# Half of the clipped products of a dense attention made on GpSimd, with a third buffer of exponentials

## The chip, the cores and the metric

One core of one Trainium2 chip. The metric is the device time of the kernel in microseconds (us). The core has five engines with queues of their own: TensorE (PE in the profile, PEld for its weight loads), VectorE (DVE), ScalarE (ACT), GpSimd (POOL) and SyncE (SP). They are ordered among each other by semaphores alone.

## The reference

Four graph networks in a row on 3125 nodes with 64 features and 100000 edges. Only the last one matters here, an attention over the edges:

```python
h = _leaky_relu(feats)
z = h @ W
el, er = z @ attn_l, z @ attn_r
e = _leaky_relu(el[src] + er[dst])                      # leaky with slope 0.2
emax = jax.ops.segment_max(e, dst, num_segments=n)
ex = jnp.exp(e - emax[dst])
denom = jax.ops.segment_sum(ex, dst, num_segments=n)
alpha = ex / jnp.where(denom == 0, 1.0, denom)[dst]
rst = jax.ops.segment_sum(alpha[:, None] * z[src], dst, num_segments=n)
return rst + bias
```

## The kernel before

Earlier phases compute the first three networks and leave in SBUF `adj3`, a dense table of edge counts: for each block of 128 source nodes (25 blocks, index `sx`), how many edges lead from each of the 128 sources (partitions) to each of the 3200 padded destination nodes (columns), in bf16. The last phase, the one that is changed, makes the attention dense: it goes through all pairs of source and destination, and the count of a pair is its weight, zero where there is no edge.

The destinations are cut into 5 chunks of 640 columns (`NCH`, `CW`), index `i`. Each chunk has 25 steps, one for each source block, so a step has the number t = 25 i + sx, from 0 to 124. A step runs over four engines:

- ScalarE (L1499, L1502) makes two exponentials of 128 x 640: `E1[t % 2]` in PSUM, of el + er minus the maximum, and `E2[t % 2]` in SBUF, of the same with the slope of 0.2. The first waits until the larger of step t - 2 is made (`mx`), the second until the product of step t - 2 is made (`mu`).
- VectorE, `larger(t)` (L1601): `E2 = max(E1, E2)`, which is the exponential of the leaky sum. One input is in PSUM, the other in SBUF.
- VectorE, `counted(t)` (L1609): `XB[t % 2] = min(E2, 2) * adj3`, both inputs in SBUF, f32 and bf16, the result f32. It waits until TensorE is done with step t - 2 (`mm`), since XB has two buffers.
- TensorE (L1539): five products of a 128 x 128 piece of XB with the 65 columns of `Z[:, sx]` (64 features and a one), added up in PSUM over the 25 steps of the chunk. In the profile each is two records, 10 a step.

Beside the steps VectorE prepares the next chunk's maxima, spread over the first 22 steps (`TURN`): `maximum(i + 1, v)` (L1574) is a running maximum MN of min(counts, a scaled el), both inputs in SBUF, 25 of them on 22 steps, so that three steps have two. In step 22 `reduce_maxima` (L1580 to L1583) reduces what TensorE has transposed (L1517, `turn_maxima`), TensorE spreads the result again (L1523, L1524, `spread_maxima`), and in step 23 `shifts` (L1592 to L1595) makes the next chunk's inputs to the exponentials. TensorE has these in a fixed order between its steps: transposes before step 21, spread before step 22. `divide` (L1616 to L1621) finishes the previous chunk in step 2.

VectorE's order in a step is written out by hand: product of step t - 1, then the maxima, then the larger of step t. GpSimd has one instruction in the whole phase, the addition of the bias (L1488).

The lines about the changed part:

Of the kernel before, what the change touches and what calls it, by code (L numbers as in the profile page):

```python
# [5 lines left out]
P = 128  # L6
NB = (N + P - 1) // P
# [39 lines left out]
f32, i32, u16, bf16 = mybir.dt.float32, mybir.dt.int32, mybir.dt.uint16, mybir.dt.bfloat16  # L47
ALU = mybir.AluOpType
ACT = mybir.ActivationFunctionType
# [27 lines left out]
@contextmanager  # L77
def phase(nc, names):

    with ExitStack() as c:  # L80
        sems = {n: c.enter_context(nc.semaphore(n)) for n in names.split()}
        with nc.Block() as block:
            yield block, sems
        nums = sorted(s.num for s in sems.values())
        at = [k for k in range(len(nums)) if not k or nums[k] != nums[k - 1] + 1] + [len(nums)]
        for k in range(len(at) - 1):
            nc.gpsimd.sem_clear(range(nums[at[k]], nums[at[k + 1] - 1] + 1))
        nc.all_engine_barrier()
# [9 lines left out]
def share(n, k, of):  # L98

    return range(n * k // of, n * (k + 1) // of)  # L100
# [27 lines left out]
def build(nc, a, out):  # L128
# [9 lines left out]
    with ctx:  # L138
        sb = lambda n, s, d: ctx.enter_context(nc.sbuf_tensor(n, s, d))
        LOW, HIGH = NB * NP // 2, 8400  # L140
        arena = sb("arena", [P, LOW + HIGH], f32)
        adj3 = arena[:, 0:LOW].bitcast(bf16).rearrange("p (s n) -> p s n", n=NP)
        al = sb("al", [P, 784], f32)
        e32 = sb("e32", [P, NB, D32], f32)
# [2 lines left out]
        identz = sb("identz", [P, 2 * P], bf16)  # L147
        identb = identz[:, 0:P]
        stage = sb("stage", [P, 2000], f32)
        adj_t = nc.dram_tensor("edge_counts", (P, NB * NP), bf16).ap()  # L150
        ps = ctx.enter_context(nc.psum_tensor("ps", [P, 8 * 512], f32))
        got = [ctx.enter_context(nc.semaphore(f"gathered{k}")) for k in range(LEAD)]
# [3 lines left out]
        def V(off, *shape, dt=f32, parts=P):  # L156

            n = 1
            for s in shape:
                n *= s  # L160
            words = n if dt in (f32, i32) else (n + 1) // 2
            v = arena[0:parts, off:off + words]
            if dt != f32:
                v = v.bitcast(dt)
            if n % 2 and dt not in (f32, i32):
                v = v[:, 0:n]
            if len(shape) == 2:
                v = v.rearrange("p (a b) -> p a b", b=shape[1])
            if len(shape) == 3:
                v = v.rearrange("p (a b c) -> p a b c", b=shape[1], c=shape[2])  # L170
            return v

        def A(off, *shape, dt=f32, parts=P):

            return V(LOW + off, *shape, dt=dt, parts=parts)
# [1283 lines left out]
        CW = 5 * P  # L1459
        NCH, TURN = 5, 22  # L1460
        E1 = [ps[:, 1024 * k:1024 * k + CW] for k in range(2)]
        MEL = ps[:, 2048:2048 + CW]
        EOS = [ps[:, 3072 + 512 * k:3072 + 512 * k + 5 * (D + 1)] for k in range(2)]
        E2 = [e32[:, :, :].rearrange("p a b -> p (a b)")[:, 0:CW], A(6450, CW)]
        X1 = [ERT[:, CW * k:CW * (k + 1)] for k in range(NCH)]
        X2 = [A(6450 + CW * (1 + k), CW) for k in range(2)]
        XB = [A(CW * k, CW) for k in range(2)]
# [3 lines left out]
        MC, OC, LIM, SPAN = [al[:, o:o + n] for o, n in ((770, 5), (776, 5), (781, 2), (783, 1))]  # L1471
        EL2, SEL = A(1600, NB), e32[:, :, :].rearrange("p a b -> p (a b)")[:, CW:CW + NB]
        LIMS = e32[:, :, :].rearrange("p a b -> p (a b)")[0:1, 700:702]
        with phase(nc, "lim lims limb sel mn1 st mn t1 dg t2 xr ex mx mu mm oc bl b3 wr") as (block, s):
            @block.sync
            def _(sp):
                sp.dma_start(B3, a["L3_gnn_bias"].rearrange("(o n) -> o n", o=1).to_broadcast([P, D])).then_inc(s["bl"], 16)
# [7 lines left out]
            @block.gpsimd  # L1485
            def _(pool):
                pool.wait_ge(s["bl"], 16)
                pool.tensor_tensor(XS, XS, B3.unsqueeze(1).to_broadcast([P, NB, D]), ALU.add).then_inc(s["b3"], 1)  # L1488

            @block.scalar  # L1490
            def _(act):
                act.wait_ge(s["sel"], 1)
                for i in range(NCH):
                    act.wait_ge(s["xr"], i + 1)
                    for sx in range(NB):
                        t = i * NB + sx
                        if t >= 2:
                            act.wait_ge(s["mx"], t - 1)
                        act.activation(E1[t % 2], X1[i], ACT.Exp, bias=EL[:, sx:sx + 1])  # L1499
                        if t >= 2:  # L1500
                            act.wait_ge(s["mu"], t - 1)
                        act.activation(E2[t % 2], X2[i % 2], ACT.Exp, bias=EL2[:, sx:sx + 1]).then_inc(s["ex"], 1)  # L1502

            @block.tensor
            def _(pe):
                pe.wait_ge(s["lim"], 1)
                for q in range(2):
                    ins = pe.transpose(ps[0:1, 3072 + q * P:3072 + (q + 1) * P], LIM[:, q:q + 1], identf[:, :])
                ins.then_inc(s["lims"], 1)
                pe.wait_ge(s["limb"], 1)  # L1510
                pe.matmul(ps[:, 3584:3586], ONE[0:1, :], LIMS, start=True, stop=True).then_inc(s["lims"], 1)

                def turn_maxima(i):

                    pe.wait_ge(s["mn"], NB * (i + 1))
                    for c in range(5):
                        ins = pe.transpose(MEL[:, c * P:(c + 1) * P], MN[:, c * P:(c + 1) * P], identf[:, :])  # L1517
                    ins.then_inc(s["t1"], 1)

                def spread_maxima(i):  # L1520

                    pe.wait_ge(s["dg"], i + 1)
                    pe.matmul(MEL[:, 0:512], ONE, DGN[:, 0:512], start=True, stop=True)  # L1523
                    pe.matmul(MEL[:, 512:CW], ONE, DGN[:, 512:CW], start=True, stop=True).then_inc(s["t2"], 1)  # L1524

                turn_maxima(0)
                spread_maxima(0)
                for i in range(NCH):
                    for sx in range(NB):
                        t = i * NB + sx  # L1530
                        if i + 1 < NCH and sx == TURN - 1:
                            turn_maxima(i + 1)
                        if i + 1 < NCH and sx == TURN:
                            spread_maxima(i + 1)
                        if sx == 0 and i >= 2:
                            pe.wait_ge(s["oc"], i - 1)
                        pe.wait_ge(s["mu"], t + 1)
                        for c in range(5):
                            ins = pe.matmul(EOS[i % 2][:, c * (D + 1):(c + 1) * (D + 1)], XB[t % 2][:, c * P:(c + 1) * P], Z[:, sx],  # L1539
                                            start=sx == 0 and c == 0, stop=sx == NB - 1, skip_group_check=True)  # L1540
                        ins.then_inc(s["mm"], 1)

            @block.vector
            def _(dve):
                st = Steps(dve, s["st"])
# [17 lines left out]
                def clear(i):  # L1563

                    if i:
                        dve.wait_ge(s["t2"], i)
                    dve.memset(MN, 0.0).then_inc(s["mn1"], 1)  # L1567
# [30 lines left out]
                def larger(t):  # L1598

                    dve.wait_ge(s["ex"], t + 1)  # L1600
                    dve.tensor_tensor(E2[t % 2], E1[t % 2], E2[t % 2], ALU.max).then_inc(s["mx"], 1)  # L1601

                def counted(t):

                    i, sx = t // NB, t % NB
                    dve.wait_ge(s["mx"], t + 1)
                    if t >= 2:
                        dve.wait_ge(s["mm"], t - 1)
                    dve.scalar_tensor_tensor(XB[t % 2], E2[t % 2], 2.0, adj3[:, sx, i * CW:(i + 1) * CW], ALU.min, ALU.mult)\  # L1609
                        .then_inc(s["mu"], 1)  # L1610

                def divide(i):
# [15 lines left out]
                for i in range(NCH):  # L1628
                    nxt = i + 1 < NCH
                    if nxt:  # L1630
                        clear(i + 1)
                    for sx in range(NB):
                        t = i * NB + sx
                        if t:
                            counted(t - 1)
                        if i and sx == 2:
                            divide(i - 1)
                        if nxt and sx < TURN:
                            for v in share(NB, sx, TURN):
                                maximum(i + 1, v)  # L1640
                        if nxt and sx == TURN:
                            reduce_maxima(i + 1)
                        if nxt and sx == TURN + 1:
                            shifts(i + 1)
                        larger(t)
                counted(NCH * NB - 1)
                divide(NCH - 1)

# [35 lines left out]
```

## Time and profile before

| | |
|---|---|
| Median of 3 runs | 4718.8 us (4710.01 to 4724.73) |
| Profiled execution: span from the first to the last instruction | 4719.8 us |
| Last phase, in the span | from about 4340 us to the end |
| First step (first L1601) | 4384.8 us |
| Last chunk's first step | 4655 us |
| Mean granted TensorE clock from 4384 to 4720 us | 0.51 |

The profile gives no time of the profiled execution apart from its span; the span is 1.0 us above the median of the runs. It is read here by its groups of instructions (duration and idle time of each line) and, for the order within a step, by its timeline. A share of busy time over the whole span says nothing on this phase, which is 8% of it.

### The profile page before, as it was taken

The numbers are of one execution on the slowest core, as the hardware profiler recorded it, in microseconds if no ns is written. First come the engines' busy times: TensorE is split into PE (matmuls) and PEld (weight loads), VectorE is DVE, ScalarE is ACT, GpSimd is POOL, SyncE is SP. The second block draws the span as 40 slices with busy tenths as digits, with TensorE's granted clock in tenths as the row PEclk, the third lists the DMA queues.
The fourth block names the chain that finished last, engine by engine and source line by source line (L and its number), as shares of the span: only waits on it lengthen the run. The fifth ranks groups of instructions, "written<-read, shape, count | busy, mean of one in ns | idle before, by whom it ended". The sixth has DMA issues, their size and how long they took to land. (4 is left out here: it accounts for less than half of the span.)

```text
span 4719.8 us, 91070 instructions
## 1 busy us (share of the span) xinstructions
PE 3468.1 (73%) x24128; PEld 3020.2 (64%) x24128; DVE 3236.7 (69%) x10293; ACT 2427.2 (51%) x8514; POOL 2503.7 (53%) x2592
## 2 busy tenths in 40 slices
PE   3767666666667776666656777777775799996789
PEld 2556555555555555555555766767675799996788
DVE  7677767677657777677764777778785433354998
ACT  0766666666275766666627666656542100000555
POOL 5777777676277777777617777777752100000000
PEclk9687888888667878888866888888875899997555
DMA  3344444444143444444414444444423200000000
GB/s 78 100 101 104 106 113 122 113 121 110 51 99 96 109 103 115 114 120 121 111 49 98 103 105 104 104 99 108 101 63 105 94 2 2 2 1 1 2 3 3
DMA packets 576845, 384.28 MB, mean 81 GB/s; under 512 B 421913, under 2 KB 498833, under 8 KB 576343
## 3 DMA queue, kind: packets, MB, share of 16 engines
q1 hardware_dynamic: 373463, 151.17, 12.5%
q0 software_dynamic: 81344, 84.68, 9.8%
q10 hardware_dynamic: 121536, 142.57, 9.8%
q8 instruction: 213, 3.49, 0.3%
q14 instruction: 289, 2.37, 0.2%
HBM read 312.87 MB, written 65.24 MB: 80 GB/s over the span
## 5 line engine op out<-in xcount | busy, mean ns | idle before, releaser
L617 POOL DMA_INDIRECT arena<-node_table,arena x1660 | 1601.7, 965 | 604.4 <-issue 474.0
L772 PE MATMUL ps<-arena 128*128 128x129 f32 x4980 | 943.9, 320 | 187.1 <-DVE arena L922 103.0
L681 ACT ACTIVATE arena<-arena 128x129 f32<-128x129 f32 x2490 | 742.7, 300 | 451.2 <-DVE arena L890 443.9
L772 PEld LDWEIGHTS ps<-arena 128*128 128x128 f32 x4980 | 788.0, 225 | 274.0 <-DVE arena L922 138.0
L919 DVE TENSOR_SCALAR arena<-arena 128x128 f32<-128x128 uint16 x2490 | 883.3, 361 | 88.7 <-PE ps L772 37.8
L617 POOL DMA_INDIRECT arena<-last_node_table,arena x830 | 793.2, 956 | 281.6 <-issue 235.3
L890 DVE TENSOR_TENSOR arena<-ps,arena 128x258 f32<-128x258 f32 x1245 | 524.7, 421 | 591.2 <-PE ps L761 244.8
L1208 PE MATMUL ps<-arena 128*128 128x192 bf16 x6875 | 587.0, 247 | 12.7 <-DVEq L1368 4.9
L1208 PEld LDWEIGHTS ps<-arena 128*128 128x128 bf16 x6875 | 584.7, 98 | 14.6 <-issue 7.4
L761 PE MATMUL ps<-arena 128*128 x2496 | 503.4, 335 | 106.1 <-ACT e L671 37.6
L761 PE MATMUL ps<-arena,e 128*128 x2484 | 494.6, 331 | 110.5 <-DVE arena L890 52.2
L798 PE MATMUL ps<-stage,al 128*128 128x400 bf16 x1190 | 357.0, 387 | 259.2 <-ACT al L689 111.6
L761 PEld LDWEIGHTS ps<-arena 128*128 128x128 f32 x2496 | 423.4, 233 | 173.1 <-issue 156.4
L761 PEld LDWEIGHTS ps<-arena,e 128*128 128x128 f32 x2484 | 410.5, 228 | 179.6 <-issue 162.7
L681 ACT ACTIVATION_READ_ACCUMULATOR arena<-arena 128x1 f32 x2490 | 468.2, 188 | 0.0
L932 DVE TENSOR_TENSOR arena<-arena,ps 128x129 f32 (+1 forms) x1245 | 363.6, 292 | 119.4 <-issue 50.5
L668 ACT ACTIVATE arena<-arena 128x256 f32<-128x256 bf16 x624 | 313.1, 502 | 138.0 <-PE ps L761 40.2
L668 ACT ACTIVATE e<-arena 128x256 f32<-128x256 bf16 x621 | 310.4, 500 | 112.3 <-PE ps L761 38.6
L1488 POOL TENSOR_TENSOR stage<-stage 128x1600 f32<-128x1600 f32 x1 | 3.6, 3552 | 656.3 <-DMA stage<-in_L_gnn_bias 656.3
L908 DVE TENSOR_SCALAR stage<-arena 128x400 bf16<-128x400 uint16 x1190 | 343.2, 329 | 0.0
L1539 PE MATMUL ps<-arena 128*128 128x65 f32 x1250 | 289.5, 420 | 33.8 <-DVE arena L1609 33.8
L1539 PEld LDWEIGHTS ps<-arena 128*128 128x128 f32 x1250 | 273.0, 329 | 51.0 <-DVE arena L1609 50.3
(338 smaller groups left out, 4625.5 us busy)
## 6 DMA issues: line engine op xcount, KB each, us to landing
arena<-in_attr SPq DMA_DIRECT2D x1245, 96.0 KB, 2.2
arena<-slot_rows ACTq DMA_DIRECT2D x249, 320.0 KB
edge_counts<-al ACTq DMA_DIRECT2D x397, 100.0 KB
arena<-node_table,arena POOLq DMA_INDIRECT x1660
edge_counts<-stage ACTq DMA_DIRECT2D x198, 100.0 KB
arena<-last_node_table,arena POOLq DMA_INDIRECT x830
arena<-edge_counts SPq DMA_DIRECT2D x24, 500.0 KB
stage<-edge_counts SPq DMA_DIRECT2D x16, 500.0 KB
```

Of the source, the lines that this page charges most:

```text
L617: pool.indirect_dma_start(out=RING[:, t % R_SLOTS, XO:XO + XG], out_offset=None, in_=table[:, :], in_offset=bass.IndirectOffsetOnAxis(ap=I ...
L668: act.activation(o, ROWB[r % 2][:, (j % 5) * BT * P:(j % 5 + 1) * BT * P], ACT.Square, bias=pid1, scale=-1.0)\
L681: ins = act.activation(PR[j % 3][:, q], PR[j % 3][:, q], ACT.Copy, accum_out=AL[w % 2][:, c:c + 1])
L761: ins = pe.matmul(UPS[j % 2][:, q * AB:(q + 1) * AB], OHT[j % 6][:, q * P:(q + 1) * P], U[:, bass.ds(b, 1), :].rearrange("p a b -> p (a b) ...
L772: ins = pe.matmul(BPS[j % 2][:, 0:AB], WOH[j % 2][:, q], RING[:, r + q, D32:D32 + AB], start=q == 0, stop=q == BT - 1)
L798: ins = pe.matmul(WPS, LOH[k % 3][:, q], KOH[k % 3][q], start=q == 0, stop=t == 0 and q == G4 - 1)
L890: dve.tensor_tensor(PR[j % 3], UPS[j % 2].rearrange("p (a b) -> p a b", b=AB), RING[:, r:r + BT, D32:D32 + AB], ALU.mult).then_inc(s["pr"], 1)
L908: ins = dve.tensor_scalar(KOH[k % 3][q], iota1[:, 0:NB * WIN], KEY4[:, adj0 + k, q:q + 1], None, ALU.is_equal)
L919: ins = dve.tensor_scalar(WOH[j % 2][:, q], iota1[:, 0:P], DZT[:, t:t + 1], PT[w % 2][:, c:c + 1], ALU.is_equal, ALU.mult)
L932: dve.tensor_tensor(to, to, BPS[j % 2], ALU.add).then_inc(s["add"], 1)
L1208: last = pe.matmul(ps[:, o + 256 * c:o + 256 * c + 3 * D], adj3[:, sx, bass.ds((d0 + c) * P, P)], g3[:, sx].rearrange("p a b -> p (a b)"), ...
L1539: ins = pe.matmul(EOS[i % 2][:, c * (D + 1):(c + 1) * (D + 1)], XB[t % 2][:, c * P:(c + 1) * P], Z[:, sx], start=sx == 0 and c == 0, stop= ...
```

## The change

Products of odd steps move from VectorE to GpSimd, where each is two operations: a clip to between 0 and 2 in place in E2 (`tensor_scalar`), a wait for it (`cl`), and the product with the counts (`tensor_tensor`), which writes `XB[1]` and increments `mp`. VectorE keeps the even ones, which all go to `XB[0]` and increment `mu`. E2 gets a third buffer, and ScalarE's second exponential waits for the product of step t - 3, whichever engine makes it. TensorE waits for `mp` or `mu` by the parity of the step.

```diff
+        third = sb("third", [P, 640], f32)
...
-        E2 = [e32[:, :, :].rearrange("p a b -> p (a b)")[:, 0:CW], A(6450, CW)]
+        E2 = [e32[:, :, :].rearrange("p a b -> p (a b)")[:, 0:CW], A(6450, CW), third[:, :]]
...
             def _(pool):
                 pool.wait_ge(s["bl"], 16)
                 pool.tensor_tensor(XS, XS, B3.unsqueeze(1).to_broadcast([P, NB, D]), ALU.add).then_inc(s["b3"], 1)
+                for t in range(1, NCH * NB, 2):
+                    i, sx = t // NB, t % NB
+                    pool.wait_ge(s["mx"], t + 1)
+                    pool.tensor_scalar(E2[t % 3], E2[t % 3], 2.0, 0.0, ALU.min, ALU.max).then_inc(s["cl"], 1)
+                    pool.wait_ge(s["cl"], t // 2 + 1)
+                    if t >= 2:
+                        pool.wait_ge(s["mm"], t - 1)
+                    pool.tensor_tensor(XB[1], E2[t % 3], adj3[:, sx, i * CW:(i + 1) * CW], ALU.mult).then_inc(s["mp"], 1)
...
+                def rows_free(t):
+
+                    if t >= 3:
+                        act.wait_ge(s["mp"] if (t - 3) % 2 else s["mu"], (t - 3) // 2 + 1)
+
...
-                        if t >= 2:
-                            act.wait_ge(s["mu"], t - 1)
-                        act.activation(E2[t % 2], X2[i % 2], ACT.Exp, bias=EL2[:, sx:sx + 1]).then_inc(s["ex"], 1)
+                        rows_free(t)
+                        act.activation(E2[t % 3], X2[i % 2], ACT.Exp, bias=EL2[:, sx:sx + 1]).then_inc(s["ex"], 1)
...
-                        pe.wait_ge(s["mu"], t + 1)
+                        pe.wait_ge(s["mp"] if t % 2 else s["mu"], t // 2 + 1)
...
-                    dve.tensor_tensor(E2[t % 2], E1[t % 2], E2[t % 2], ALU.max).then_inc(s["mx"], 1)
+                    dve.tensor_tensor(E2[t % 3], E1[t % 2], E2[t % 3], ALU.max).then_inc(s["mx"], 1)
...
-                    dve.scalar_tensor_tensor(XB[t % 2], E2[t % 2], 2.0, adj3[:, sx, i * CW:(i + 1) * CW], ALU.min, ALU.mult)\
+                    dve.scalar_tensor_tensor(XB[0], E2[t % 3], 2.0, adj3[:, sx, i * CW:(i + 1) * CW], ALU.min, ALU.mult)\
                         .then_inc(s["mu"], 1)
...
-                        if t:
+                        if t % 2:
                             counted(t - 1)
```

## Rows read from the trace of the kernel before

**Rows 1.** The page: span, and the lines of the chain that ended last.

```profile
span 4719.8 us, 91070 instructions
...
PE ps L1539 3%; DVE al L1574 1%; DVE e L1601 1%; DVE arena L1601 1%; DVE arena L1609 0%; PE ps L1523 0%; PE ps L1517 0%; DVE al L1593 0%; DVE al L1592 0%; DVE arena L1594 0%; DVE arena L1595 0%; DVE e L1560 0%; DVE al L1567 0%; PE ps L1524 0%; DVE arena L1619 0%
```

**Rows 2.** Groups from 4160 us on: busy us, mean ns of one | idle before, releaser.

```profile
L1539 PE MATMUL ps<-arena 128*128 128x65 f32 x1250 | 289.5, 420 | 33.8 <-DVE arena L1609 33.8
...
L1574 DVE SCALAR_TENSOR_TENSOR al<-arena,e,al 128x640 f32<-128x640 bf16 x125 | 110.0, 880 | 3.9
L1499 ACT ACTIVATE ps<-arena,dis 128x640 f32<-128x640 f32 x125 | 99.7, 797 | 105.1 <-DVE arena L1601 52.9 <-DVE e L1601 52.3
L1502 ACT ACTIVATE e<-arena 128x640 f32<-128x640 f32 x63 | 52.1, 828 | 9.9 <-DVE arena L1609 7.1
```

**Rows 3.** Timeline, VectorE in one step with an M: start us, duration us.

```profile
4389.61 0.82 DVE L1601 TENSOR_TENSOR e<-ps,e 128x640 f32<-128x640 f32 x1
4390.46 0.83 DVE L1609 SCALAR_TENSOR_TENSOR arena<-e,arena 128x640 f32<-128x640 f32 x1
...
4391.20 0.88 DVE L1574 SCALAR_TENSOR_TENSOR al<-arena,e,al 128x640 f32<-128x640 bf16 x1
...
4392.00 0.82 DVE L1601 TENSOR_TENSOR arena<-ps,arena 128x640 f32<-128x640 f32 x1
```

**Rows 4.** Timeline and windows of TensorE in the last chunk (busy us, count, clock).

```profile
4657.16 57.86 PE L1539 MATMUL ps<-arena 128*128 128x65 f32 x270 [3.49 <-DVE arena L1609]
...
4655.00:4720.00 65.00, 57.86 (x270) 57.67 (x270) 45.08 (x63) 38.48 (x50) 0.00 (x0) 0.51 0.02 5
```

**Rows 5.** GpSimd by line (ns min/median/max), by timeline (L1488) and by group (L328).

```profile
L624 POOL TENSOR_TENSOR arena<-arena x15: 723/724/949, 1238.0 to 3601.2; 128x320 f32<-128x320 f32 x15
...
L625 POOL TENSOR_TENSOR arena<-arena x15: 747/751/877, 1238.8 to 3602.0; 128x320 f32<-128x320 f32 x15
...
L1119 POOL COPY arena<-arena x8: 1847/1854/3245, 3620.6 to 3680.1; 128x2000 bf16<-128x2000 bf16 x8
...
4343.10 3.55 POOL L1488 TENSOR_TENSOR stage<-stage 128x1600 f32<-128x1600 f32 x1 [656.30 <-DMA stage<-in_L_gnn_bias]
...
L328 POOL TENSOR_SCALAR_AFFINE_SELECT identz<-identz 128x128 bf16<-128x128 bf16 x1 | 0.4, 408 | 0.0
...
L328 POOL TENSOR_SCALAR_AFFINE_SELECT identf<-identf 128x128 f32<-128x128 f32 x1 | 0.3, 292 | 0.2 <-POOL identz L325 0.2
```

**Rows 6.** Timeline at a convolution's end, VectorE and GpSimd at once.

```profile
1242.22 0.75 POOL L625 TENSOR_TENSOR arena<-arena 128x320 f32<-128x320 f32 x1
...
1242.62 0.49 DVE L1021 TENSOR_TENSOR arena<-ps,arena 128x320 f32<-128x320 f32 x1 [4.30 <-PE ps L861]
1243.15 0.72 POOL L624 TENSOR_TENSOR arena<-arena 128x320 f32<-128x320 f32 x1 [0.18 <-POOL arena L625]
...
1243.25 0.97 DVE L1024 TENSOR_TENSOR arena<-arena 128x320 f32<-128x320 f32 x1
...
1243.95 0.88 POOL L625 TENSOR_TENSOR arena<-arena 128x320 f32<-128x320 f32 x1
1244.26 0.76 DVE L1028 TENSOR_SCALAR arena<-arena 128x320 f32<-128x320 f32 x1
...
1248.30 0.49 DVE L1024 TENSOR_TENSOR arena<-arena 128x320 f32<-128x320 f32 x1
```

**Rows 7.** Timeline of TensorE and VectorE in the turn of chunk 3.

```profile
4645.84 1.27 PE L1517 MATMUL ps<-identf,al 128*128 128x128 f32 x5
4646.15 0.82 DVE L1609 SCALAR_TENSOR_TENSOR arena<-e,arena 128x640 f32<-128x640 f32 x1
...
4647.15 0.82 DVE L1580 TENSOR_REDUCE al<-ps 128x5 f32<-128x640 f32 x1 [0.17 <-PE ps L1517]
...
4649.46 2.08 PE L1523 MATMUL ps<-al 128*128 128x512 f32 x2
...
4652.00 0.82 DVE L1592 TENSOR_TENSOR al<-ps,arena 128x640 f32<-128x640 f32 x1 [1.00 <-PE ps L1524]
```

More of the change, by code:

```diff
@@ L1473, in build @@
         LIMS = e32[:, :, :].rearrange("p a b -> p (a b)")[0:1, 700:702]
-        with phase(nc, "lim lims limb sel mn1 st mn t1 dg t2 xr ex mx mu mm oc bl b3 wr") as (block, s):
+        with phase(nc, "lim lims limb sel mn1 st mn t1 dg t2 xr ex mx mu mp cl mm oc bl b3 wr") as (block, s):
             @block.sync
```

## The prediction

> **What bounds the kernel now.** I read the page first: one execution with a span of 4719.8 us, and a chain that ends in the last phase, with the sums of L1539, the maxima of L1574, the larger exponential of L1601 and the clipped product of L1609 [rows 1]. The change lies wholly in that phase, so nothing of the earlier phases can move. I then took the groups of the phase [rows 2] and the timeline. Three engines run in a ring, 125 times. Call the steps t = 0..124. For a step, ScalarE makes two exponentials, L (L1601, VectorE) takes the larger, C (L1609, VectorE) clips and multiplies it, TensorE sums it in 10 recorded matmuls; in the first 22 steps of chunks 0 to 3 VectorE also makes M (L1574), the running maximum of the next chunk.
>
> In such a step with one M, VectorE starts L at 4389.61, C 0.85 us later, M 0.74 after C, and the next L 0.80 after M: 2.39 us a step, no gap [rows 3]. ScalarE needs 0.80 + 0.83 us, TensorE 2.14 (57.86 us for 270 matmuls, 27 steps) at the granted clock of 0.51, which is the 1.2 GHz level [rows 2, 4]. So VectorE bounds the steps with an M, with TensorE only 0.25 us behind it, and TensorE bounds the last chunk, where it has no gap over those 57.86 us [rows 4].
>
> **What the change removes.** 62 of the 125 C go from VectorE. Of these, 44 are in steps with an M (88 such steps in four chunks), 12 in the last chunk, 6 in the turns between chunks. Where VectorE is the bound a pair of steps (o odd, e even) would fall from 2 x 2.39 = 4.78 us to 4.78 - 0.74 = 4.04. TensorE allows no less than 2 x 2.14 = 4.28.
>
> **What it adds on GpSimd.** For each odd step a clip (one input, 640 columns), a wait for its own end, and a product (two inputs, of which one is bf16). The product: 320 columns take 724 and 751 ns (medians), 1600 take 3.55 us, so 2.2 ns a column above 320, and 640 columns come to 0.74 + 320 x 0.0022 = 1.44 us [rows 5]. Its upper bound: the one operation on GpSimd with both a bf16 and a f32 form took 408 against 292 ns for 128 columns, 0.9 ns a column, which on 640 would make 2.0 us [rows 5]. The clip has no row. The nearest single-input row is the copy of 2000 columns in 1.854 us, 0.93 ns a column: 0.59 us, and some 0.1 for its start, 0.70 us; the lower bound is 0.59, the upper that of a product, 1.44. I take 0.70, since a clip reads one tensor as the copy does. Between one GpSimd instruction and the next that waits for it I take 0.08 us (the product that ends at 1243.87 is followed by one at 1243.95) [rows 6].
>
> The Trainium skill, GPSIMD Engine Reference, section 3.1, gives 1.03 cycles per element at 1.2 GHz for bodies of up to two operations. By that the clip is an estimated 0.55 us, and the pair below 0.15 us shorter; no row here shows a clip.
>
> **The port.** The rows that decide are those of the end of a convolution, where GpSimd and VectorE work at once [rows 6]. L1024, a VectorE operation with two SBUF inputs, takes 0.49 us alone (1248.30) and 0.97 when it starts 0.10 after a GpSimd product; it ends at 1244.22, 0.35 us after that product's end at 1243.87. L1028 stretches in the same way to 0.76. L1021, with one input from PSUM, starts inside a GpSimd product (1242.22 to 1242.97) and takes 0.49, what L1024 takes alone for the same size. The GpSimd product that starts at 1243.95, while L1024 is still at work, takes 0.88 instead of 0.75. (L1028 has one SBUF input, and a GpSimd product holds it too.) So a VectorE operation with two SBUF inputs and a GpSimd product don't overlap; 0.14 us of VectorE's start are hidden in the wait (0.49 - 0.35). Here C (E2 and the counts) and M (the counts and MN) have two SBUF inputs, L (PSUM and E2) has not.
>
> The Trainium skill, SBUF — State Buffer, section "SBUF: two separate sides", says that the pair of ports is held exclusively for a whole instruction, and the loser fully blocks. The trace agrees on the blocking but shows 0.14 us of the start hidden; with nothing hidden the pair below would be 5.42 and not 5.28 us.
>
> **The pair afterwards.** Put time 0 at the end of a product on GpSimd for which C waits. C is done at 0.69 (0.83 - 0.14), M starts at 0.60, L(o) at 1.40, M at 2.25, L(e) at 3.05, and VectorE comes to the next C at 3.90. GpSimd: the clip of o is issued at about 2.3, when L(o) is done, but M, which stands directly behind L on VectorE, has the port till 3.13. Clip to 3.83 or, with some of its start hidden, 3.76; product from 3.84. Who is first at 3.9? C(e) also waits for TensorE to be done with the only even XB: the odd step's matmuls can start at 0.05, take 2.14, the even one's another 2.14, so C is not free before 4.37. The product wins by half a microsecond, holds the port to 5.28, and C waits for it. The pair is thus 5.28 us: VectorE's 4.04, and 1.44 for the product, less the 0.14 hidden and some overlap. In words: a C of 0.74 us is taken off VectorE and a blockade of 1.44 us, during C, is put on it. ScalarE has slack (3.26 us in the pair; the third E2 lets it run ahead, and the odd product is done before its buffer is wanted). Cost: 44 x (5.28 - 4.78) = 22 us.
>
> **The turns.** TensorE now gets odd data late, and the turn of the maxima is queued behind it. Before, the transposes (L1517, 1.27 us) ended 0.17 us after VectorE wanted them, 1.00 us after C began at 4646.15, and the shifts (L1592) began 5.85 us after that C, 2.5 after TensorE began the spread [rows 7]. In chunks 1 and 3, TensorE begins step 20 only at the end of the product, is done at 2.19, transposes until 3.5, and VectorE waits for that; TensorE's step 21 then ends at 5.65, and the spread (2.5 us) at 8.2: +2.4 us each. In chunks 0 and 2 two steps (4.33) lie before the transposes, but a C less on VectorE, and the shifts start at 10.3 instead of 9.2: +1.1 each. Together 7 us. VectorE's removed 6 C are worth nothing there, because VectorE waits for TensorE in just those places. The 12 second M's of a step cost a little less than now (about -1 us), as GpSimd's clip or product can pass between; the start of the last chunk costs 1 us, as its first odd product comes late.
>
> **The last chunk.** No M. After L(o): 0.1 + 0.70 + 0.1 + 1.44 to the odd data. The ring C and L(o) (1.6), clip and product (2.3), two steps of TensorE (4.37) closes over two pairs in 8.3 us, 4.15 a pair, below TensorE's 4.28: nothing changes, the cover being TensorE. With a clip of 1.44 us it would be 4.5 a pair, +3 us.
>
> The third buffer, the two semaphores and GpSimd's bias addition (over at 4346.65, long before the first odd step) [rows 5] cost nothing that lies on the path. Sum: 22 + 7 + 1 = 30 us on the profiled execution of 4719.8, whose time is within 1 us of the median 4718.8: 4749 us, +0.6%.
>
> **Rivals.**
> 1. *The forecast*: product 1.44, clip 0.6 to 0.8, port exclusive. +16 to +40 us. For it: in one window both VectorE rows without a PSUM input that meet a GpSimd product are stretched to its end, and the one with PSUM is not [rows 6]. Chance 0.58.
> 2. *GpSimd's operations are slow* (bf16 operand, two-operation clip). With a product of 2.0 us the pair is 5.84, +47 and the turns: 4774. With a clip of 1.44 the product is ready at 4.6, behind C at 4.37; C goes first, the product holds back the M behind it, and the next C waits longer for TensorE: pairs of about 4.4 and 7.6 alternate, 6.0 on average, +54 and the turns: 4780. For it: neither form has a row. Against: other GpSimd rows fit one price per column. Chance 0.17.
> 3. *The port doesn't matter for these shapes* (the other side). M or C against GpSimd overlap. Then the ring decides: C to the end of the product 2.39 + 0.09 + 0.70 + 0.10 + 1.44 = 4.72, two steps of TensorE 4.37, over two pairs: 4.55 a pair, 44 x 0.23 = 10 us less, and up to 6 less for the 12 second M's, whose pair was 5.78 and has slack now: 4703. It decides once M and C keep 0.88 and 0.83 us beside GpSimd. Against it: L1024 has the same kind of operands, f32 in both; M's counts are bf16, which is all that speaks for it. Chance 0.10.
> 4. *The blockade is partly hidden*: C is put between clip and product, or the product falls on both L. The pair lies between 4.6 and 5.1, -8 to +14 us. Against: the wait of C for TensorE (4.37) works for the product. Chance 0.15.
>
> **How the numbers follow.** 0.3% is 14 us; less can hardly be told from no change here. Slower by more: cases 1 and 2, 0.75. Within: case 4 and part of 3, 0.19. Faster by more: the rest of 3, 0.06. The range leaves out 3 and the far end of 2 (both prices slow at once): 4712 to 4785. The forecast's own range is 4734 to 4759.
>
> **What would show it.** In the changed profile: even C of 1.5 us or more instead of 0.83 in chunks 0 to 3, and 0.83 in the last; L unchanged at 0.82; a pair of 5.2 to 5.4 us; GpSimd products of 1.44 us; L1539's stretch in the last chunk still 2.14 a step; longer waits of L1580 and L1592 for TensorE. Wrong would be the forecast if C and M keep their lengths beside GpSimd (case 3), if the clip is much over 1 us (case 2), or if the pair is near 4.6 (case 4).

## The result and the profile after

The changed kernel takes 4734.84 us (median of 12 runs, 4731.6 to 4743.99) against 4717.6 us for the kernel before (12 runs, 4707.06 to 4735.38). The ratio is 1.0041, with a 95% interval from 1.0031 to 1.0052: slower by 17 us in the medians, 19 us by the ratio. 4749 was forecast, with 4712 to 4785 as the range. The direction and its cause were right; the cost was put too high, at 30 us.

The page and the groups of the last phase (busy us, mean ns | idle before, releaser) answer to [rows 1] and [rows 2]. L1588 is now M, L1615 L, L1623 C; L1493 is GpSimd's clip, L1497 its product, L1553 TensorE's sums:

```profile
span 4742.2 us, 91132 instructions
...
PE ps L1553 3%; DVE al L1588 1%; POOL arena L1497 1%; POOL e L1493 0%; DVE e L1615 0%; POOL third L1493 0%; PE ps L1537 0%; DVE third L1615 0%; POOL arena L1493 0%; DVE arena L1615 0%; PE ps L1531 0%; DVE al L1597 0%; DVE al L1607 0%; DVE al L1606 0%; DVE al L1594 0%
...
L1553 PE MATMUL ps<-arena 128*128 128x65 f32 x1250 | 279.8, 418 | 61.4 <-POOL arena L1497 48.2 <-DVE arena L1623 13.1
```

TensorE's sums, which waited 33.8 us for VectorE's products, wait 48.2 us for GpSimd's and 13.1 for VectorE's. GpSimd is new in the chain. From the first larger to the end of the span, the **stage** in what follows, 335.0 us have become 353.7: +18.7. The other 3.7 us of the two spans' difference lie before that point, in phases that the change doesn't touch.

The durations by line (ns min/median/max), and the timeline of a pair of steps:

```profile
L1493 POOL TENSOR_SCALAR third<-third x20: 719/1282/1286, 4401.8 to 4722.1; 128x640 f32<-128x640 f32 x20
...
L1497 POOL TENSOR_TENSOR arena<-third,arena x20: 1393/1396/2439, 4403.2 to 4722.9; 128x640 f32<-128x640 f32 x20
...
L1623 DVE SCALAR_TENSOR_TENSOR arena<-arena x21: 824/1045/1972, 4399.2 to 4733.2; 128x640 f32<-128x640 f32 x21
...
L1615 DVE TENSOR_TENSOR e<-ps,e x42: 809/812/824, 4388.5 to 4729.7; 128x640 f32<-128x640 f32 x42
...
4399.16 1.04 DVE L1623 SCALAR_TENSOR_TENSOR arena<-arena 128x640 f32<-128x640 f32 x1 [0.96 <-PE ps L1553]
...
4399.58 4.53 PE L1553 MATMUL ps<-arena 128*128 128x65 f32 x20 [0.53 <-POOL arena L1497]
4400.13 0.87 DVE L1588 SCALAR_TENSOR_TENSOR al<-arena,e,al 128x640 f32<-128x640 bf16 x1
4400.92 0.81 DVE L1615 TENSOR_TENSOR third<-ps,third 128x640 f32<-128x640 f32 x1
4401.66 0.87 DVE L1588 SCALAR_TENSOR_TENSOR al<-arena,e,al 128x640 f32<-128x640 bf16 x1
...
4401.82 1.28 POOL L1493 TENSOR_SCALAR third<-third 128x640 f32<-128x640 f32 x1 [2.30 <-DVE third L1615]
4402.45 0.81 DVE L1615 TENSOR_TENSOR e<-ps,e 128x640 f32<-128x640 f32 x1
...
4403.19 1.40 POOL L1497 TENSOR_TENSOR arena<-third,arena 128x640 f32<-128x640 f32 x1
...
4404.22 1.04 DVE L1623 SCALAR_TENSOR_TENSOR arena<-e,arena 128x640 f32<-128x640 f32 x1 [0.96 <-PE ps L1553]
```

To be seen: the pair goes from 4399.16 to 4404.22, 5.06 us, where two steps of [rows 3] took 4.78. The clip is issued 0.16 us after M has started (M at 4401.66), stands behind it for the 0.71 us until M ends and is done 0.57 us after that; by itself a clip takes 0.72, the group's minimum. The product starts 0.09 us after the clip and ends at 4404.59. C may start at 4404.22 by TensorE's leave, but ends only 0.67 us after the product: 1.04 us instead of 0.83. L stays at 0.81 with the clip at work beside it.

### The profile page after: what moved, and what is told of

Its sections match the earlier page's. It is cut to its first block and busy times, and to the rows that moved or that the text cites. A ratio compares the mean times of both kernels' runs of the same rounds, so it can differ in the third digit from the quotient of the medians.

```text
span 4742.2 us, 91132 instructions
## 1 busy us (share of the span) xinstructions
PE 3460.8 (73%) x24128; PEld 3016.9 (64%) x24128; DVE 3210.8 (68%) x10231; ACT 2420.3 (51%) x8514; POOL 2661.4 (56%) x2716
## 5 line engine op out<-in xcount | busy, mean ns | idle before, releaser
L1553 PE MATMUL ps<-arena 128*128 128x65 f32 x1250 | 279.8, 418 | 61.4 <-POOL arena L1497 48.2
L1553 PEld LDWEIGHTS ps<-arena 128*128 128x128 f32 x1250 | 270.1, 330 | 71.8 <-POOL arena L1497 57.9
```

## The experiments

They ran on three chips (e1 to e4 on one, e5 to e8 on a second, e9 and e10 on a third), on which the phases before this one take about 1000 us longer: the kernel before takes 5729 to 5770 us there. Why they do was not looked into. The stage takes the same time, at a granted TensorE clock of 0.50 to 0.51 in every run (335.1 us in e4, whose code differs from the kernel before in one buffer), so each result is read from its stage in the profiled execution, in us, and from the ratio of its runs to those of the kernel before on the same chip. The stage comes from one execution of each kernel. It repeats well: steps 0 to 20 of the chunks, which are the same in the kernel before, e4 and e9, differ by at most 0.03 us a chunk. The ratios are coarser, about 0.1% or 6 us to either side.

**e1: the port alone.** All products on VectorE as before; GpSimd works beside it on a buffer nobody reads.

```diff
+                pool.memset(third[:, :], 1.0).then_inc(s["cl"], 1)
+                for t in range(1, NCH * NB, 2):
+                    i, sx = t // NB, t % NB
+                    pool.wait_ge(s["mx"], t + 1)
+                    pool.wait_ge(s["cl"], t // 2 + 1)
...
+                    pool.tensor_scalar(third[:, :], third[:, :], 2.0, 0.0, ALU.min, ALU.max).then_inc(s["cl"], 1)
+                    pool.wait_ge(s["cl"], t // 2 + 2)
+                    pool.tensor_tensor(third[:, :], third[:, :], adj3[:, sx, i * CW:(i + 1) * CW], ALU.mult).then_inc(s["mp"], 1)
```

> This is the kernel before, VectorE making all 125 products, with GpSimd doing a clip and a product of the same size (640 columns, f32 and bf16 counts) for every odd step on a buffer of its own, for which nobody waits. Theory A (the shared port): VectorE's M or C waits for GpSimd's product; a pair of steps with an M rises from 4.78 to about 5.9 us, +40 to +60 us in all, and C or M is seen at up to 2 us. Theory B (only the late odd data, through TensorE, cost time): nothing changes, within 5 us of the kernel before, C 0.83 and M 0.88 us.

Measured: ratio 1.0076 (1.0058 to 1.0093), +44 us; the stage is 378.1, +43.1. Timeline of a pair (L is L1613, C L1621, M L1586):

```profile
5443.41 0.83 DVE L1621 SCALAR_TENSOR_TENSOR arena<-arena 128x640 f32<-128x640 f32 x1
...
5443.47 1.35 POOL L1497 TENSOR_SCALAR third<-third 128x640 f32<-128x640 f32 x1 [3.30 <-DVE arena L1613]
5444.16 1.34 DVE L1586 SCALAR_TENSOR_TENSOR al<-arena,e,al 128x640 f32<-128x640 bf16 x1
...
5444.90 1.85 POOL L1499 TENSOR_TENSOR third<-third,arena 128x640 f32<-128x640 f32 x1
5445.42 0.81 DVE L1613 TENSOR_TENSOR e<-ps,e 128x640 f32<-128x640 f32 x1
5446.27 1.17 DVE L1621 SCALAR_TENSOR_TENSOR arena<-e,arena 128x640 f32<-128x640 f32 x1
...
5449.00 0.83 DVE L1621 SCALAR_TENSOR_TENSOR arena<-arena 128x640 f32<-128x640 f32 x1
```

GpSimd's work, on which nobody waits, stretches M from 0.87 to 1.34 us and every second C from 0.83 to 1.17; the pair takes 5.59 instead of 4.78 us, and 0.47 + 0.34 = 0.81 is that difference. Theory B falls. Over 44 pairs it is 36 of the 43 us. The price per pair is less than the 1.1 I had in mind, for part of the product runs under L. Also new: the clip, issued during C, gets in between C and the M that stands directly behind it (C ends at 5444.24, the clip at 5444.82, M at 5445.50).

**e5: late odd data without the port.** GpSimd's operations only write: this kernel leaves out the odd products, and TensorE sums a constant in their place.

```diff
-                    pool.tensor_scalar(E2[t % 3], E2[t % 3], 2.0, 0.0, ALU.min, ALU.max).then_inc(s["cl"], 1)
...
-                    pool.tensor_tensor(XB[1], E2[t % 3], adj3[:, sx, i * CW:(i + 1) * CW], ALU.mult).then_inc(s["mp"], 1)
+                    for k in range(3):
+                        if k:
+                            pool.wait_ge(s["cl"], 2 * (t // 2) + k)
+                        pool.memset(XB[1], 0.5).then_inc(s["mp"] if k == 2 else s["cl"], 1)
```

> The changed kernel, with GpSimd's clip and product replaced by three memsets of the odd buffer, one after the other, which read nothing from SBUF; TensorE sums the constant for the odd steps, so the odd products are left out. TensorE gets its odd data about as late as in the changed kernel (1.9 instead of 2.1 us after the larger), the ring of waits is the same. Theory A (port, which only readers of SBUF on GpSimd block): C keeps 0.83 and M 0.87 us, the pair falls from 5.06 to TensorE's 4.55 to 4.65 us, the stage from the first larger to the end from 353.7 to 329 to 336 us. Theory B (late odd data in the ring): the pair stays at 4.9 or more, the stage at 348 us or more.

Measured: ratio 0.9993 (0.9981 to 1.0004); the stage is 332.1, 21.6 us below the changed kernel. In its timeline (M is L1589, C L1624):

```profile
5566.73 0.88 DVE L1589 SCALAR_TENSOR_TENSOR al<-arena,e,al 128x640 f32<-128x640 bf16 x1
...
5566.87 2.01 POOL L1498 MEMSET arena<- 128x640 f32 x3 [2.86 <-DVE third L1616]
5567.52 0.82 DVE L1616 TENSOR_TENSOR e<-ps,e 128x640 f32<-128x640 f32 x1
...
5568.71 0.82 DVE L1624 SCALAR_TENSOR_TENSOR arena<-e,arena 128x640 f32<-128x640 f32 x1 [0.37 <-PE ps L1554]
```

The memsets overlap with M, C starts 0.17 us before the last of them ends, and both keep their lengths, 0.88 and 0.82 us. A pair takes 4.58 us here. TensorE gets the odd data 2.1 us after the larger's end. In the changed kernel it is 2.9 (4401.73 to 4404.59), for there the clip stands behind M for 0.71 us; so e5 shows that data 2.1 us late cost nothing outside the turns, and what the rest of the lateness does is left to e3. The last chunk took 69.0 us against 65.8 in the changed kernel; here all three memsets wait for TensorE to free the odd buffer, where in the changed kernel the clip doesn't: a flaw of this experiment that hides 3 us more of gain.

**e3: a second buffer for the even products**, from chunk 1 on.

```diff
-        XB = [A(CW * k, CW) for k in range(2)]
+        XB = [A(0, CW), A(CW, CW), ERT[:, 0:CW]]
+        of = lambda t: 1 if t % 2 else 2 if t > NB and t % 4 == 2 else 0
...
-                        dve.wait_ge(s["mm"], t - 1)
+                        dve.wait_ge(s["mm"], t - 3 if t > NB else t - 1)
```

> The changed kernel with a second buffer for the even products from chunk 1 on, so that C no longer waits for TensorE to finish the last even step. Theory A (port): C and GpSimd's product still can't overlap; whichever is first, the pair stays at 4.9 to 5.2 us, within 6 us of the changed kernel. Theory B (C waits for TensorE in the ring): the pair falls to TensorE's pace of 4.55 in three of the four chunks, -15 us or more.

Measured: ratio 1.0035 (1.0023 to 1.0048); the stage is 353.1 against 353.7. From chunk 1 on the wait for TensorE is gone, and C waits for the port in its place (C is L1624):

```profile
5552.82 1.40 POOL L1498 TENSOR_TENSOR arena<-third,arena 128x640 f32<-128x640 f32 x1
5552.93 1.97 DVE L1624 SCALAR_TENSOR_TENSOR arena<-e,arena 128x640 f32<-128x640 f32 x1
...
5557.88 1.32 POOL L1498 TENSOR_TENSOR arena<-arena 128x640 f32<-128x640 f32 x1
```

C starts 0.11 us behind the product, takes 1.97 us, and the pair stays at 5.06 (5552.82 to 5557.88). The odd data are as late here as in the changed kernel. So neither their lateness nor the 0.96 us for which C "waits for PE" in the changed kernel sets the pair.

**e4: the third buffer alone.** The kernel before with E2[t % 3] and ScalarE waiting for the product of step t - 3.

> The kernel before with a third buffer of exponentials alone. Both theories: VectorE bounds the steps with an M and TensorE the last chunk, ScalarE waits for nobody who matters: within 3 us of the kernel before. If it gains, the third buffer has paid for part of GpSimd's cost in the change.

Measured: ratio 0.9998 (0.9985 to 1.0011); the stage is 335.1. It is worth nothing by itself.

**e2: the clip taken from GpSimd.** The larger clips E1 in its own instruction; E2, the exponential of the 0.2 slope, is no longer clipped for the odd steps, which matters only where it would overflow.

```diff
-                    dve.tensor_tensor(E2[t % 3], E1[t % 2], E2[t % 3], ALU.max).then_inc(s["mx"], 1)
+                    dve.scalar_tensor_tensor(E2[t % 3], E1[t % 2], 2.0, E2[t % 3], ALU.min, ALU.max).then_inc(s["mx"], 1)
...
-                    pool.tensor_scalar(E2[t % 3], E2[t % 3], 2.0, 0.0, ALU.min, ALU.max).then_inc(s["cl"], 1)
-                    pool.wait_ge(s["cl"], t // 2 + 1)
```

> The changed kernel without GpSimd's clip: VectorE's larger clips the first exponential at 2 in the same instruction (min, then max), so the GpSimd product follows it directly. Theory A (port): the product runs under the second larger and the wait for TensorE, ends about 0.6 us before C is wanted, and a pair falls from 5.06 to 4.55 to 4.65 us, TensorE's own pace: -18 to -26 us against the changed kernel, 4708 to 4717 us, 0 to 8 us below the kernel before. Rival (each GpSimd product costs VectorE its 1.4 us wherever it is): the pair stays at 4.9 or more and the gain is under 7 us.

Measured: ratio 1.0 (0.9988 to 1.0012); the stage is 328.2, 25.5 below the changed kernel and 6.8 below the one before. The ratio alone doesn't tell e2 from the kernel before: 6.8 us are 0.12%, the end of its interval. The pair is no longer one number but goes between some 4.3 and 4.8 us. L with the clip takes 0.81 us as before, and C is back at its length (L is L1613, C L1621):

```profile
L1621 DVE SCALAR_TENSOR_TENSOR arena<-e,arena x21: 824/826/1176, 5431.2 to 5741.2; 128x640 f32<-128x640 f32 x21
...
5454.52 0.83 DVE L1621 SCALAR_TENSOR_TENSOR arena<-arena 128x640 f32<-128x640 f32 x1 [0.95 <-PE ps L1551]
...
5456.96 1.97 POOL L1495 TENSOR_TENSOR arena<-third,arena 128x640 f32<-128x640 f32 x1 [2.86 <-DVE third L1613]
5457.59 0.82 DVE L1613 SCALAR_TENSOR_TENSOR e<-ps,e 128x640 f32<-128x640 f32 x1
...
5458.79 0.83 DVE L1621 SCALAR_TENSOR_TENSOR arena<-e,arena 128x640 f32<-128x640 f32 x1 [0.38 <-PE ps L1551]
```

The product stands behind M for 0.71 us, then runs under L and is nearly done when TensorE lets C go. So it is not GpSimd's product as such that costs: with the clip ahead of it, it fell upon C.

**e6: GpSimd only in steps 0 to 15 of chunks 0 to 3**, and **e7: the turn one step earlier in TensorE's order**, each on top of e2; **e8** has both. The edit of e7:

```diff
-                        if i + 1 < NCH and sx == TURN - 1:
+                        if i + 1 < NCH and sx == TURN - 2:
                             turn_maxima(i + 1)
-                        if i + 1 < NCH and sx == TURN:
+                        if i + 1 < NCH and sx == TURN - 1:
                             spread_maxima(i + 1)
```

That of e6:

```diff
+        on_pool = lambda t: t % 2 == 1 and t < (NCH - 1) * NB and t % NB <= 15
...
-                for t in range(1, NCH * NB, 2):
+                for t in [v for v in range(NCH * NB) if on_pool(v)]:
...
-                        if t % 2:
+                        if t and not on_pool(t - 1):
                             counted(t - 1)
```

> As the kernel whose larger clips (e2), but GpSimd makes odd products only in steps 0 to 15 of chunks 0 to 3; VectorE makes the others, the last chunk's too. If TensorE's lag at the turn cost e2 its gain there, the stage goes from 328.2 to 325 to 328 us although three pairs in a chunk are again at 4.78; the last chunk is 64.5 us as before. If the turn was no matter it is 329 to 331.

> e2 with the transposes and the spread of the maxima one step earlier in TensorE's order (before steps 20 and 21 instead of 21 and 22). Theory of the turns (they wait behind TensorE's late steps): VectorE's waits for them fall from about 3.1 to under 1.5 us a chunk, the stage from 328.2 to 320 to 326 us. If the wait is only moved to TensorE, which then stands idle for the last maximum, the stage stays within 1 us.

> e6 and e7 together. If both gains are of the same wait they don't add: 321 to 327 us for the stage, 8 to 14 us less than the kernel before in all.

Measured: e6 ratio 0.9989 (0.9979 to 0.9999), stage 326.7; e7 0.9981 (0.9969 to 0.9992), stage 322.0; e8 0.9983 (0.9972 to 0.9995), stage 325.5. By the stage e7 is the fastest, 13.0 us less than the kernel before, with a median of 5725.03 against 5737.11 us; the ratios of e6, e7 and e8 overlap and don't rank them. VectorE's waits for TensorE in e7 (us in total, times, longest): L1592 waits for the transposes, hardly any more; L1604 waits for the spread, 5.7 us as in the changed kernel; L1621 is C. The two together are 1.8 us a chunk, where under 1.5 was expected:

```profile
DVE arena L1621 <- PE ps L1551: 38.9, 35, 2.0
DVE al L1604 <- PE ps L1536: 5.7, 4, 1.9
...
DVE al L1592 <- PE ps L1529: 1.4, 2, 0.7
```

e8's stage is 3.5 us above that of e7; of these, 2.6 us lie in steps 0 to 20 of the four chunks, where pairs went back to VectorE, and 1.7 in the turns, less 0.8 that the last chunk gives back.

**e9 and e10: the edit of e7 in the kernel before and in the changed one.**

> The kernel before, all products on VectorE, with the transposes and the spread one step earlier in TensorE's order, as in e7. If e7's gain over e2 (6.2 us of the stage) is due to TensorE's lag behind GpSimd's products, the kernel before gains little by the same edit: the stage 331 to 335 us (335.0 before). If it is a gain that any version has, 328 to 331.

> The changed kernel with the same edit of TensorE's order. Theory of the turns: about 8 us of the changed kernel's cost lie in waits for TensorE there (VectorE's 10.7 + 5.7 us for the transposes and the spread against 0.7 + 4.0 before); the stage falls from 353.7 to 345 to 350 us and stays 10 us or more above 335.0, since the pairs keep their 5.06 us. If the turns cost nothing of their own it stays at 353.

Measured: e9 ratio 1.0006 (0.9996 to 1.0017), stage 333.8; e10 1.0021 (1.0011 to 1.0031), stage 345.2. In the changed kernel the edit is worth 8.5 us, in the one before 1.2. So some 7 us of the changed kernel's cost were TensorE's lag at the turns.

## Why the prediction was right, and where it was off

**The port: right, and shown.** With GpSimd's operations and no one waiting for them the kernel before loses 43 us of stage (e1); without reads from SBUF, and data 2.1 instead of 2.9 us late, the changed kernel loses nothing outside the turns (e5); and with the full lateness, but C free of TensorE, it still loses all but 0.6 us of what it lost (e3). What L1024 and L1021 showed [rows 6] carried over: operations with two SBUF inputs wait for GpSimd's end, bf16 counts or not, and finish 0.67 us after it (0.69 was reckoned from 0.14 us hidden); the one that reads PSUM goes on. Rival 3 is out, since M and C don't keep their lengths beside GpSimd. The changed profile shows the blockade less plainly than the forecast had it: it wanted an even C of 1.5 us or more and a pair of 5.2 to 5.4, and got 1.04 and 5.06. C is short because TensorE lets it go late, at 4.70 instead of 4.37, when only 0.37 us of the product are left. A pair of 5.06 lies in the range that rival 4 had for a partly hidden blockade, and the forecast's own range (4734 to 4759) was met at its lower end; what speaks for the forecast's mechanism is e3, where C has 1.29 us of the product ahead of it and the pair is the same.

**The pair: 5.06 us, not 5.28.** This is the term that was mis-sized, 12 us in place of 22. From the end of one product to the next, three steps were shorter. M starts 0.74 us after L, not 0.85: I took the spacing from L to C [rows 3] for that from L to M, an order that the kernel before never has. The clip ends 0.57 us after M, where 0.63 was reckoned: 0.15 us of its 0.72 are hidden in the wait, not 0.07 of 0.70. The product takes 1.40 instead of 1.44. Together 0.12 + 0.06 + 0.04 = 0.22. The bf16 operand costs nothing extra, so rival 2 is out. The order was as forecast: the product beats C, for C waits for TensorE; TensorE's two steps took 4.53 us from a standing start, not 2 x 2.14, and let C go at 4.70, not 4.37. e3 shows that the pair is the same without that wait; C then starts 0.11 us after the product, so the order hung on a tenth of a microsecond there.

**The turns: right, a little low.** The wait for the transposes grew as worked out. The first two lines are the turn of chunk 3 after, the next two the waits (us in total, times, longest):

```profile
4668.25 0.83 DVE L1594 TENSOR_REDUCE al<-ps 128x5 f32<-128x640 f32 x1 [2.87 <-PE ps L1531]
...
4673.10 0.82 DVE L1606 TENSOR_TENSOR al<-ps,arena 128x640 f32<-128x640 f32 x1 [1.86 <-PE ps L1538]
...
DVE al L1594 <- PE ps L1531: 10.7, 4, 2.9
...
DVE al L1606 <- PE ps L1538: 5.7, 4, 1.9
```

Before, these were 0.17 and 1.00 us in chunk 3 [rows 7]. The shifts start 8.4 us after the product's end at 4664.70; 8.2 was forecast. In chunks 0 and 2 it is 10.5, and 10.3 was forecast. Against 5.85 and 9.2 before, the four turns are some 7.7 us longer by the forecast's own marks; it had 7. e10 recovers 8.5, of which 1.2 are there in the kernel before too.

**The second M's of a step** give more than the 1 us put down: where the second M stands behind L(o), GpSimd's clip passes between the two, and that pair takes 5.43 us (product's end 4420.69 to 4426.12), 0.37 above the others, where before it took 1.00 more; where it stands behind C it costs 0.91 (4404.59 to 4410.56). Over 12, six of each kind, that is some 4 us. The pair of 5.43 us (L1588 stands here for both M's):

```profile
4419.29 1.40 POOL L1497 TENSOR_TENSOR arena<-third,arena 128x640 f32<-128x640 f32 x1
...
4422.82 2.12 DVE L1588 SCALAR_TENSOR_TENSOR al<-arena,e,al 128x640 f32<-128x640 bf16 x2
...
4424.35 1.77 POOL L1497 TENSOR_TENSOR arena<-arena 128x640 f32<-128x640 f32 x1
```

**The last chunk** costs 1.3 us (65.82 against 64.52 from the last shift to the end), 1 was forecast. The sum of the terms as measured: 44 x 0.28 = 12.3, 1.3, less some 4 for the second M's, leaves 9 of the 18.7 us for the turns. The traces agree: from the larger of step 20 to the next chunk's first larger the four turns are 2.8, 1.9, 2.8 and 1.7 us longer than before, 9.2 together, steps 0 to 20 of the four chunks 7.5 and the last chunk from its first larger 2.0. (Where pairs end and a turn begins is a matter of the mark: the blockade of step 20 counts to the turn here.)

**The third buffer** costs nothing and gains nothing by itself (e4).

The Trainium skill, SBUF — State Buffer, section "SBUF: two separate sides", limits the contention of a VectorE instruction with two SBUF inputs to GpSimd operations that read SBUF. The trace agrees: beside the memsets of e5, M takes 0.88 us, behind the clip of e1 1.34.

## What to carry over

A VectorE operation that is taken to GpSimd must be priced as a blockade, not by the engine's free time: in these traces every VectorE operation with two SBUF inputs (M, C, L1024) stands until the GpSimd operation that reads SBUF is done, and GpSimd's stand behind M and C in the same way. Here 0.74 us were taken away and 1.40 put in their place. It paid where GpSimd's operation fell beneath work that reads PSUM or beneath a wait, as in e2 and e7, where one short operation less turned +18.7 us of stage into -6.8 and, with TensorE's queue put in order behind it, into -13. And where an engine's input is made later, look for what is queued behind it: the turns cost some 9 us here, the pairs 12.

## What the runs showed of the hardware that was not expected

- GpSimd gets its turn between two VectorE instructions that follow without a gap: in e1 the clip waits 0.77 us for C, and M, directly behind C, then waits for the clip.
- The clip, a `tensor_scalar` with two operations on 128 x 640 f32, takes 0.72 us on GpSimd, a memset of the same size 0.63, the product of f32 and bf16 1.40 when E2 lies in a tensor of its own and 1.32 when it lies in the arena. What makes these 0.08 us wasn't tried.
- In the changed kernel GpSimd's bias addition fell on VectorE's first M, which took 3.55 us; in the kernel before it fell on a 25-column operation in front of it (L1560, 3.3 us). VectorE loses 2.7 us by it after and 3.0 before: the cost changes its place and hardly its size.
